# Attention scores as float32r products of two heads in the two halves of the array's rows, and P.V in one step, in a two-layer transformer kernel

## The reference

```python
x = L0_attn_x
xn = _layernorm(x, axis=-1)
x = x + _L0_attn_ref(xn, ...) + _L0_ffn_ref(xn, ...)
xn = _layernorm(x, axis=-1)
x = x + _L1_attn_ref(xn, ...) + _L1_ffn_ref(xn, ...)
...
scores = jnp.einsum('bhqd,bhkd->bhqk', q, k)
weights = softmax(causal(scores) / HD ** 0.5)
ctx = jnp.einsum('bhqk,bhkd->bhqd', weights, v)
```

## Time and profile before

| | before |
|---|---|
| median of 3 runs | 942.08 us (941.6 to 943.6) |
| profiled execution | 943.2 us, its span 941.6 us |
| TensorE (matmul) busy | 887.2 us, 94% |
| VectorE, GpSimd, ScalarE busy | 524.5, 497.5, 458.0 us |
| mean granted TensorE clock | 0.98 of full speed |

### The profile page before, as it was taken

One profiled execution on the slowest core, in us unless ns is written; L12 is line 12 of the kernel. 1 busy time (PEld: TensorE's weight loads), 2 busy tenths in 40 slices (PEclk: granted clock), 3 DMA queues, 4 the chain that ended last, 5 costly groups with the idle time before them and its releaser, 6 DMA issues. The chain is left out here.

```text
span 941.6 us, 16765 instructions
## 1 busy us (share of the span) xinstructions
PE 887.2 (94%) x5790; PEld 645.2 (69%) x5790; DVE 524.5 (56%) x1543; ACT 458.0 (49%) x838; POOL 497.5 (53%) x747
## 2 busy tenths in 40 slices
PE   6778999999999899999999999999999999999887
PEld 3654655666788666677678886677667876566677
DVE  5455454756756656644576566545476474454353
ACT  2343444545646435444475555444375454344542
POOL 6834445453565534555555665455455666454343
PEclk7889999999999999999999999999999999999999
DMA  6534151523241421527172642827344463721131
GB/s 190 123 106 105 41 119 36 119 68 87 77 89 58 108 68 47 119 84 154 57 145 71 148 95 75 159 67 136 90 113 106 107 140 106 149 63 61 54 90 35
DMA packets 62146, 91.01 MB, mean 97 GB/s; under 512 B 9104, under 2 KB 31120, under 8 KB 62064
## 3 DMA queue, kind: packets, MB, share of 16 engines
q1 hardware_dynamic: 62064, 89.95, 39.6%
HBM read 77.21 MB, written 12.71 MB: 95 GB/s over the span
## 5 line engine op out<-in xcount | busy, mean ns | idle before, releaser
L921 POOL TENSOR_TENSOR w_lo<-w_raw,w_hi 128x512 fp32r<-128x512 f32 x204 | 268.3, 1320 | 84.6 <-ACT w_hi L988 80.8
L981 ACT ACTIVATE p<-s_ring 128x512 f32<-128x512 f32 x320 | 183.4, 597 | 175.2 <-PE s_ring L1381 174.5
L1213 DVE CUSTOM_DVE_ANT_0 s_ring<-s_ring,causal 128x384 f32<-128x384 f32 (+3 forms) x512 | 239.0, 515 | 48.1 <-PE s_ring L1358 47.2
L968 POOL TENSOR_SCALAR_AFFINE_SELECT p<-p 128x256 f32<-128x256 f32 (+1 forms) x320 | 121.0, 381 | 255.2 <-ACT p L981 252.8
L1245 PE MATMUL g_ring<-xt_hi,w_hi 128*128 128x512 f32 (+1 forms) x504 | 214.4, 425 | 6.8 <-DVE xt_lo L1143 3.1
L1245 PE MATMUL g_ring<-xt_lo,w_hi 128*128 128x512 f32 (+1 forms) x504 | 200.2, 397 | 0.0
L1245 PE MATMUL g_ring<-xt_hi,w_lo 128*128 128x512 f32 (+1 forms) x504 | 199.6, 396 | 0.0
L988 ACT ACTIVATE w_hi<-w_raw 128x512 fp32r<-128x512 f32 x204 | 127.6, 627 | 51.0 <-PE acc L1245 25.0
L1381 PE MATMUL s_ring<-q_op,k_op 99*128 99x384 bf16 (+3 forms) x512 | 118.8, 304 | 12.3 <-DVE maxima L1213 6.2
L1245 PE MATMUL acc<-w_hi,h_hi 128*128 128x256 f32 (+1 forms) x400 | 123.3, 308 | 4.1 <-DVE h_lo L1194 4.1
L1358 PE MATMUL s_ring<-k_op,q_op 96*128 96x384 bf16 (+3 forms) x512 | 115.8, 303 | 8.9 <-DVE maxima L1213 4.5
(11 more groups left out here) (86 smaller groups left out, 1138.9 us busy)
## 6 DMA issues: line engine op xcount, KB each, us to landing
w_raw<-weights_in SPq DMA_DIRECT2D x204, 256.0 KB, 2.7
q_op<-qk_scratch SPq DMA_DIRECT2D x96, 128.0 KB, 4.4
qk_scratch<-qk_parts SPq DMA_DIRECT2D x26, 384.0 KB, 2.6
k_op<-qk_scratch SPq DMA_DIRECT2D x48, 128.0 KB, 4.3
x<-x_in SPq DMA_DIRECT2D x8, 256.0 KB, 4.5
y_out<-x SPq DMA_DIRECT2D x8, 256.0 KB, 2.6
k_op<-qk_scratch SPq DMA_DIRECT2D x24, 64.0 KB, 3.0
bo_all<-bo_in SPq DMA_DIRECT2D x2, 256.0 KB, 5.1
```

The costliest lines, as they stand in the source:

```text
L921: pool.tensor_tensor(w_lo[:, c % SPLIT, :], w_raw[:, c % RAW, :], w_hi[:, c % SPLIT, :].bitcast(F32), ALU.subtract).then_inc(split_done, 1)
L968: pool.affine_select(out=view, in_=view, compare_op=ALU.is_ge, fill=0.0, base=0, pattern=[[0, n], [1, P]] if n == 2 else [[1, P]], channel ...
L981: act.activation(p32[:, j % PRING, :], s_ring[r % SRING][:, :], ACT.Exp, scale=SCALE).then_inc(exp_done, 1)
L1213: last = dve.tensor_tensor_reduce(out=s_ring[r % SRING][:, at:at + n], in0=s_ring[r % SRING][:, at:at + n], in1=causal[:, 512 - n:], scale ...
```

## The change

The scores are computed from float32r operands: q and k are split in two parts (the high one by ScalarE, the low one by VectorE straight into `qk_parts`), and three products stand in 3 x 16 = 48 rows, with two rows for the negative maximum (its high and low part, made by two VectorE instructions after a float32 transpose). An even head of a unit lies in rows 0 to 49, an odd one in rows 64 to 113, and their matmuls are issued in turn, each into its own bank. One step `ST` (a visit) does the two score jobs 2i and 2i + 1 of a unit and the two transposed-score jobs of the unit seven visits earlier; there are 5 visits to a unit and 167 in all. A visit waits for both maxima jobs and both exponentials of the visit before. `PV` runs in one step of 16 matmuls after the unit's last mask, and into a `g_ring` bank. GpSimd's `msplit`, `qlo` and `xn`, and ScalarE's `qmid`, are gone. q and k go out in three DMAs and come back in two (layer 0's k by two for each octet of heads), the maxima in one and back in two, and four DMAs write the ones. In the prologue all twelve `xn` are VectorE's, the transposes have four banks, one more q projection stands in it, and the warm-up is 28 matmuls, with 8 more after the first four transposes.

```diff
-QROWS = 6 * HD
-MROWS = QROWS + 3
-Q_PARTS = (0, 0, 1, 0, 1, 2)
-K_PARTS = (0, 1, 0, 2, 1, 0)
+QROWS = 3 * HD
+MROWS = QROWS + 2
+ROW_TILE = 64
...
-RAW, SPLIT, HSPLIT, PRING, SRING = 4, 4, 3, 14, 3
+RAW, SPLIT, HSPLIT, PRING, EARLY_BANKS = 4, 4, 3, 14, 4
+VISITS = JOBS // 2
+LAG = VISITS + 2
+SCORE_VISITS = 4 * QUADS * VISITS
...
-HEADS = (10, 0, 0, 7)
+HEADS = (12, 0, 0, 7)
...
-PV_AT = (0.55, 0.95, 1.1)
-OTR_AT = 1.2
+PV_AT = 1.25
+OTR_AT = 1.36
...
-WARM = 22
+WARM = 28
...
+    q1 = w_octet(0, 1, 0)
+    prologue = (ln_0 + filler(0, 8) + ln_1[:1] + q + k0 + ln_1[1:3] + w_v(0, 0, 0) + ln_1[3:] + k1 + w_v(0, 1, 1) + ln_n[:3] + q1
+                + ln_n[3:] + rms_1)
...
-        q_op = sb("q_op", [MROWS, 2, 8, T], BF16)
-        k_op = sb("k_op", [MROWS, 2, 8, T], BF16)
+        q_op = sb("q_op", [P, 2, 4, T], F32R)
+        k_op = sb("k_op", [P, 2, 4, T], F32R)
...
-        s_ring = [ctx.enter_context(nc.psum_tensor(f"s_ring{i}", [P, 512], F32)) for i in range(SRING)]
+        s_bank = [ctx.enter_context(nc.psum_tensor(f"s_bank{i}", [P, 512], F32)) for i in range(2)]
+        t_bank = [ctx.enter_context(nc.psum_tensor(f"t_bank{i}", [P, 512], F32)) for i in range(2)]
...
-        pv_ps = ctx.enter_context(nc.psum_tensor("pv_ps", [P, 512], F32))
...
+        def operands(u, j):
+
+            rows = ROW_TILE * (j % 2)
+            slot, pair = u // 2 % 2, 2 * (u % 2) + j // 2
+            k_pair = u % 2 if u < 2 * QUADS else pair
+            return rows, slot, pair, k_pair
...
-                    sp.dma_start(qk_scratch[n % 2], qk_parts[:, n % 2, :, :]).then_inc(qk_out[n % 2], 16)
+                    for at in range(3):
+                        sp.dma_start(to[at * HD:(at + 1) * HD].rearrange("d h t -> h d t"),
+                                     qk_parts[:, n % 2, int(at == lo_at), :].bitcast(F32)
+                                     ).then_inc(qk_out[n % 2], 16)
...
+                    if octet >= 2:
+                        sp.wait_ge(t_made, t_count(2 * octet - 3))
+                    for half in range(2):
+                        rows = ROW_TILE * half
+                        sp.dma_start(dst[rows:rows + QROWS, octet % 2, :, :].bitcast(F32),
+                                     qk_scratch[n % 2].rearrange("r (p two) t -> two r p t", two=2)[half]
+                                     ).then_inc(here[octet % 2], 16)
...
+                elif kind == "ST":
+                    v = s[1]
+                    if v < SCORE_VISITS:
+                        u, i = divmod(v, VISITS)
+                        if i:
+                            pe.wait_ge(smax_done, max(n_smax[(u, 2 * i - 2)], n_smax[(u, 2 * i - 1)]))
...
+                        blocks = [score_blocks(job) for job in (2 * i, 2 * i + 1)]
+                        for n_block, pair in enumerate(zip(*blocks)):
+                            for j, qt, at in pair:
+                                n = (qt + 1) * P
+                                r, slot, p, kp = operands(u, j)
+                                ins = pe.matmul(s_bank[j % 2][:, at:at + n],
+                                                q_op[r:r + QROWS, slot, p, qt * P:(qt + 1) * P],
+                                                k_op[r:r + QROWS, slot, kp, 0:n], start=True, stop=True)
...
+                    if v >= LAG:
+                        t_u, i = divmod(v - LAG, VISITS)
+                        done = [JOBS * t_u + 2 * i - 2, JOBS * t_u + 2 * i - 1]
+                        if done[0] >= 0:
+                            pe.wait_ge(exp_done, max(n_exp[j] for j in done))
...
+                    for j, kt, job, at in PV_BLOCKS:
                         slot, vh = v_head(u, j)
-                        last = pe.matmul(pv_ps[32 * j:32 * j + VW, kt * P:T], v_op[:, slot, kt, vh, :],
-                                         p32[:, (JOBS * u + job) % PRING, at:at + T - kt * P],
-                                         start=kt == 0, stop=kt == 2, skip_group_check=True)
-                    last.then_inc(pv_done, 1)
+                        ins = pe.matmul(g_ring[g % 2][32 * j:32 * j + VW, kt * P:T], v_op[:, slot, kt, vh, :],
+                                        p32[:, (JOBS * u + job) % PRING, at:at + T - kt * P],
+                                        start=kt == 0, stop=kt == 2, skip_group_check=True)
```

More of the change, by code:

```diff
@@ L260, in qk_job @@
-        assert used < NEVER
-        end["qkin", n] = end[kind, octet] = place("sp", max(end["qkout", n], used), "qkin", n, kind, l, b,
-                                                  octet) + TRANSFER
+        lo = end["g", g] = place("dve", hi, "qres", n, g, kind, l, m)
+        reuse = 0.0 if l == 0 and kind == "k" else after("qkin", n - 2)
+        end["qkout", n] = place("sp", max(lo, reuse), "qkout", n, kind, l, b) + TRANSFER
+        if l == 0 and kind == "k":
+            end["k_out", b] = end["qkout", n]
+            for octet in range(8):
+                if ("q_made", octet) in end:
+                    key_load(octet)
+            return
@@ L264, in qk_ready, with key_load, load @@
+    def key_load(octet):
+        written = max(at("k_out", 0), at("k_out", 1))
+        if written == NEVER:
+            return
+        def load():
+            end["k", octet] = place("sp", max(written, slot_free(octet)), "kin", octet) + 2 * TRANSFER
+        when_free(octet, load)
     def qk_ready(kind, l, xslot, octet):
-        last = 2 * octet - 3
-        if kind == "k" and l:
-            last = {8: 7, 9: 15}.get(octet, last)
-        if (kind == "q" and octet >= 2 or kind == "k" and l) and at("T", last) == NEVER:
+        if after("qkin", state["qk"] - 2) == NEVER:
@@ new lines, in visit @@
+    def visit(v):
+        e = pe_step(visit_ready(v), "ST", v)
+        if v < SCORE_VISITS:
+            u, i = divmod(v, VISITS)
+            for job in (2 * i, 2 * i + 1):
+                end["sbank", job % 2] = end["smax", u] = place("dve", e, "smax", u, job)
+            if i < VISITS - 1:
+                end["smax", u] = NEVER
+        if v >= LAG:
+            u, i = divmod(v - LAG, VISITS)
+            if i == VISITS - 1:
+                end["T", u] = e
+                for load in waiting.pop(u, []):
+                    load()
+            for job in (2 * i, 2 * i + 1):
+                j = JOBS * u + job
+                done = end["tbank", job % 2] = place("act", max(e, p_freed(j)), "exp", j, u, job)
+                end["p", j] = place("pool", done, "mask", j, job)
@@ L375, in mtrans_ready @@
     def mtrans_ready(u):
[L376 removed]
+        return at("smax", u)
     def mtrans(u):
[L379 to L381 removed]
+        e = end["Mt", u] = pe_step(end["smax", u], "Mt", u)
+        done = end["sbank", 0] = place("dve", max(e, after("mout", u - 2)), "mrow", u)
@@ L408, in otr_ready, with pv @@
+    def pv(u):
+        g = take("g")
+        e = end["PV", u] = pe_step(max(pv_ready(u), after("g", g - 2)), "PV", g, u)
+        end["g", g] = end["oev", u] = place("act", max(e, after("otr", u - 1)), "oev", g, u)
     def otr_ready(u):
@@ L858, in _ @@
[L858 to L867 removed]
+                    sp.wait_ge(qk_out[n % 2], 48 * (n // 2 + 1))
```

559 lines of the change are left out of this document (252 added, 307 removed).

## The result

The kernel after takes 960.28 us (median of 4 runs, 956.5 to 966.0) against 942.84 us for the kernel before on the same chip: ratio 1.019, 95% interval 1.013 to 1.025. It is slower by 1.9%, where 910 us was forecast. Its profiled execution took 966.0 us.

The account below looks back on a forecast made before the run. Outside the start, time was taken as the sum of TensorE's instruction costs. P.V -11, row halves -23, start -8 and new waits +10 took the span from 941.6 to 909.6 us; forecast 910 us, range 888 to 922, chance 0.63.

Parts of the forecast that it names:

- Part 6: Other engines' work and the q and k operand DMAs: changes fit in idle time or ahead of need, costed at nothing.
- The cover that I named: Operand DMAs on SyncE's queue: they wait for unit 2o - 3, four visits (some 16 us) before octet o is needed.
- an octet without cover: Operand DMAs: without the four visits' lead an octet would cost about 5 us, 14 times.
- the warnings at the end: Signs of error: leaving halves far dearer than strips, clock below full from 80 to 880 us, SyncE's queue holding back weights.
- Part 2: Scores in row halves on TensorE: halves run side by side, visits 0.71 us, 118 us instead of 141, 23 us less.
- Part 3: Weight loads of the halves: taken at nothing; rival of one path for all loads, 41 us more, chance 0.12.
- Part 1: P.V in one step per unit on TensorE: two of three fixed costs go, 2.46 us each, 11 us less (7 to 20).
- Part 4: The start: VectorE's xn bring the first projection near 15.5 us; 8 us less in all, between 3 and 15.
- Part 5: New waits of visits for both banks, on maxima and exponentials, mostly at phase ends: +10 us, between 0 and 25.
- the sum: Whole kernel's span: 941.6 - 11 - 23 - 8 + 10 = 909.6 us, forecast as 910 us run time.

Follow-up runs that it names:

- e3: Kernel after with q and k going out in one DMA of 512 KB by 128 rows and back in six: 905.54 us, 0.960 of the kernel before.
- e9: e3 with odd heads reading the even heads' rows, so all matmuls of a visit lie in one half: 972.63 us, ratio 1.030.
- e4: Kernel before with only P.V in one step of 16 matmuls after the last mask, in its own bank: 949.24 us, ratio 1.006.
- e5: Kernel after with its three DMAs out kept and the way back in six DMAs of 128 KB: 988.12 us, ratio 1.046.
- e10: e3 with the way out in three DMAs of 256 KB, 768 KB in all, each described by 128 rows: 909.12 us, ratio 0.962.
- e12: e3 with one DRAM row left free after each head's 16, so the DMA out goes as 8 blocks: 946.27 us, ratio 1.002.
- e2: Kernel after with only the planner's operand trip durations altered, to 8.5 us out and 7.1 us back: 926.14 us, ratio 0.981.
- e8: e3 with all matmuls of the even head issued first in each visit, then all of the odd: 908.22 us, ratio 0.964.

## Why the prediction was wrong

The step that failed is in Part 6, "at nothing": "Operands: three DMAs out and two of 384 KB in replace one and six of 128 KB, 4.4 us to landing". I weighed the number of DMAs and the landing of the old ones, put the trip at no cost, and never asked how the new way out was described, nor how early k sets out. The runs showed a trip of 8.2 instead of 2.6 us, 40.0 us of waiting for k in the kernel after, and 54.7 us back when the way out is one DMA by 128 rows (e3). The cover that I named, four visits ahead of an octet, covers the wait for a free slot and not the trip: k leaves only 11.3 us before its first visit is due in the trace above. The price that I gave for an octet without cover, 5 us, was near: 31.4 us at eight octets (3.9 us each) and 8.6 us at the start. It had no term for the clock that falls behind each wait. I gave this case no rival and no chance; of the warnings at the end, only "if the clock falls below full speed between 80 and 880 us" came true, and as a consequence.

- **Row halves (Part 2):** right. Visits take 0.67 to 0.72 us against 0.71; e9 shows that the halves run together. Loads (Part 3) cost nothing, as taken, though Part 3 counted them wrongly: as the transposed jobs lag by seven visits, a unit has four visits of six matmuls and one of eight, and none of four. The sum of 32 loads to a unit is the same.
- **P.V (Part 1):** the step costs 2.28 us against 2.46. The forecast gain of 11 us depends on the order around it: by itself in the kernel before it is a loss of 6 us (e4).
- **Both together:** e3's TensorE is busy 854.8 us, 32.4 less than before, where Parts 1 and 2 gave 34. Some 3 us of it are the clock and not the two parts (TensorE is busy at 1.2 GHz for 28 us before and 23 in e3).
- **The start (Part 4):** the first projection is at 16.36 us; forecast near 15.5, before 18.33. In e3 the first 60 us hold 8.3 us more work than in the earlier trace rows; 8 was forecast. In the kernel after the wait of 8.6 us for k eats it.
- **New waits (Part 5):** +10 us forecast. The waits on maxima and their rows came to 11.4 us, about as before. The term was too large: e3 is idle for 47.9 us against 54.4 before, 6.5 less, of which the start gives 8.3, so all new waits cost about 2 us there (an estimate). e3, with a span of 902.7 us, lies 6.9 us below the sum.
- **The difference:** the measured span (963.9) lies 54.3 us above the forecast one (909.6). It is the 61.2 us between e3 and the kernel after, 40.8 of them idle and 20.4 the clock, less the 6.9 us by which e3 is below the forecast.

That the way out costs, and by its description, is shown by e3, e5, e10 and e12; the outermost dimension alone accounts for 40.7 of the 54.7 us (e12). Three things stay open: what bytes, number of DMAs and scattered rows add while the way out goes by 8 heads (e5 against e12); what two DMAs back are worth with a way out by 128 rows, a kernel that wasn't tried; and whether the kernel before would bear the slower way out, which wasn't tried either.

## What to carry to other kernels

Read a DMA's description as closely as its bytes: here an outermost dimension of 8 instead of 128 halved what was under way at once, and cost e3 40.7 us with not one byte more. Where a plan is written out by hand or by a planner, each transfer's length is part of the program: measure the trip of the new form first, since 4 us more per trip (8.2 against 3.9) turned a change worth 4% into a loss of 2%, and telling the plan the true length gave 34 us back with no faster transfer (e2). A change of layout is several changes; cost the one "at nothing" by when its result is needed.

## What the runs showed of the hardware

Leaving one row free in DRAM per 16 halved the pieces under way at once (9 to 12 against 17 to 19), raised the DMA's issue from 0.34 to 0.58 us and the trip from 3.9 to 7.0 us. Two row halves of 64 work independently enough that matmuls of different halves start out of the program's order (e8) and four weight loads take 0.30 us; the Trainium skill, page "TensorE: Matmul & The Clock Gate", section "Part 3: Packing small matmuls — row/col tiling", says that matmuls start and end strictly in program order, and the trace of e8 disagrees on the starts. After a wait of 6.5 us TensorE's clock was at 1.2 GHz for 4.7 us more. Behind the nine waits for k, of 1.8 to 8.6 us, such stretches last 3.8 to 6.2 us, 43 us in all. At half speed they lose some 22 us, an estimate that is near the 20.4 us by which the kernel after is busier than e3. Five more stretches at 1.2 GHz lie in layer 0, away from waits for k; e3 has three there.
